# Attention steps of a graph network kernel: ScalarE makes the second half of the one-hots, VectorE the first, and the clamp of the logits goes

## The reference, cut to what matters

```python
e = leaky_relu(a_src[:, src] + a_dst[:, dst] + fc_b, 0.2)   # one row for each of 4 heads
seg_max = segment_max(e, src)
e = exp(e - seg_max[:, src])
seg_sum = segment_sum(e, src)
msg = (e / seg_sum[:, src])[:, :, None] * hp[:, dst, :]
agg = segment_sum(msg, src)                                  # mean over heads, + bias
```

## Time and profile before

| what | us |
| --- | --- |
| median of 3 runs | 20600.07 |
| lowest, highest | 20592.81, 20604.26 |
| the profiled execution | 20595.7 |
| its span in the trace | 20593.9 |
| of it the attention stage, first to last message (L2221) | 6272.9 to 8603.6 |
| VectorE busy in the whole span | 17281.9 (84%) |
| GpSimd busy | 13246.4 (64%) |
| TensorE busy | 9779.6 (47%) |
| ScalarE busy | 5966.3 (29%) |

### The profile page before, as it was taken

One profiled execution on the slowest core, in us unless ns is written; L12 is line 12 of the kernel. 1 busy time (PEld: TensorE's weight loads), 2 busy tenths in 40 slices (PEclk: granted clock), 3 DMA queues, 4 the chain that ended last, 5 costly groups with the idle time before them and its releaser, 6 DMA issues.

```text
span 20593.9 us, 293981 instructions
## 1 busy us (share of the span) xinstructions
PE 9779.6 (47%) x63545; PEld 7463.1 (36%) x63546; DVE 17281.9 (84%) x25284; ACT 5966.3 (29%) x13901; POOL 13246.4 (64%) x14067
## 2 busy tenths in 40 slices
PE   0114010110016777653348777777777765336432
PEld 0114010100015666643235555555555544225322
DVE  9989999999997888787659999999999986664666
ACT  0000333333322222230004444454545445004300
POOL 0058777777777777735757777777777731770376
PEclk9655555555558888755558888888888875555555
DMA  1033444444412112174331111111111147336534
GB/s 18 0 54 24 30 35 31 33 31 32 33 22 45 36 36 36 34 242 124 84 52 12 12 12 12 12 12 12 12 12 12 12 89 230 79 77 162 181 79 68
DMA packets 1751558, 1095.98 MB, mean 53 GB/s; under 512 B 1217323, under 2 KB 1658124, under 8 KB 1750028
## 3 DMA queue, kind: packets, MB, share of 16 engines
q0 software_dynamic: 454272, 412.11, 18.2%
q1 hardware_dynamic: 1089532, 417.46, 8.2%
q10 hardware_dynamic: 207632, 265.14, 4.1%
HBM read 700.94 MB, written 391.12 MB: 53 GB/s over the span
## 4 chain that ended last, share of the span: by engine, by line
DVE 43%; DVEq 20%; issue 12%; DMA 10%; PE 10%; POOL 3%; ACT 1%; ACTq 0%; POOLq 0%; SPq 0%
DVEq L2477 11%; DMA srcs<-spread,nbx 9%; DVE arena L1750 7%; DVE arena L1749 6%; DVE srcs L2472 6%; POOL srcs L801 3%; DVE red L2478 3%; PE banks L1264 2%; DVEq L2205 2%; PE banks L1347 2%; DVE arena L1722 2%; DVE arena L2173 2%; DVE arena L1567 2%; PE banks L1405 1%; PE banks L1193 1%
## 5 line engine op out<-in xcount | busy, mean ns | idle before, releaser
L779 POOL DMA_INDIRECT gat<-tab,nbr x3328 | 3509.4, 1054 | 2151.3 <-DMA nbr<-nbr_src 1137.2
L801 POOL DMA_INDIRECT srcs<-spread,nbx x2808 | 2654.9, 945 | 2713.5 <-DMA nbx<-from_src 1375.3
L779 POOL DMA_INDIRECT gat<-tab,pay x3328 | 3176.8, 955 | 1078.4 <-issue 854.3
L1405 PE MATMUL banks<-w2rows,dsts 128*128 128x384 f32 x6656 | 3177.9, 613 | 894.1 <-DVE srcs L2472 700.2
L745 POOL DMA_INDIRECT pay<-records,nbr x2560 | 2489.7, 973 | 797.7 <-issue 780.0
L2478 DVE TENSOR_REDUCE red<-srcs 128x80 f32<-128x1280 f32 x1664 | 2474.6, 1487 | 151.4
L2173 DVE TENSOR_TENSOR arena<-arena,banks 128x96 f32 (+2 forms) x4472 | 1210.4, 271 | 1474.0 <-PE banks L1264 890.6
L1193 PE MATMUL banks<-ident,arena 128*128 128x128 f32 x2240 | 426.3, 376 | 4231.5 <-DVE arena L1750 2810.2
L1264 PE MATMUL banks<-srcs,hot 128*128 128x96 bf16 (+1 forms) x11232 | 1148.5, 278 | 2482.7 <-DMA srcs<-spread,nbx 2364.0
L906 ACT COPY banks<-arena 128x1024 f32<-128x1024 f32 (+1 forms) x1508 | 1324.5, 879 | 3299.6 <-DVE arena L1750 1275.6
L1405 PEld LDWEIGHTS banks<-w2rows,dsts 128*128 128x128 f32 x6656 | 1359.9, 227 | 1735.0 <-DVE srcs L2472 849.2
(11 more groups left out here) (394 smaller groups left out, 20741.4 us busy)
## 6 DMA issues: line engine op xcount, KB each, us to landing
spread<-srcs SPq DMA_DIRECT2D x936, 192.0 KB
dsts<-key_rows SPq DMA_DIRECT2D x234, 512.0 KB, 4.1
spread<-srcs ACTq DMA_DIRECT2D x468, 204.0 KB
staged<-gat SPq DMA_DIRECT2D x416, 148.0 KB, 1.8
gat<-staged ACTq DMA_DIRECT2D x416, 148.0 KB
dsts<-key_rows ACTq DMA_DIRECT2D x117, 512.0 KB, 4.5
gat<-tab,nbr POOLq DMA_INDIRECT x3328
gat<-tab,pay POOLq DMA_INDIRECT x3328
```

The source lines that it names most:

```text
L779: pool.indirect_dma_start(out=gatv(s, GC[pas])[:, t, :], out_offset=None, in_=TAB[pas], in_offset=bass.IndirectOffsetOnAxis(ap=row, axis=0 ...
L801: pool.indirect_dma_start(out=chunk_rows(s, c)[:, q, :], out_offset=None, in_=rows, in_offset=bass.IndirectOffsetOnAxis(ap=nbx[:, r, s * X ...
L1405: last = t_.matmul(bank[1 + 2 * (p % 2) + h][:, 0:384], hid_rows[:, s % 2, 2 * p + h, :], w2rows[:, :], start=True, stop=True)
```

## The change

VectorE compares only tiles 0 to 3 of a step (512 elements) and still signals hot_ready. ScalarE makes tiles 4 to 7 in `second_hots`: it copies the four keys into an f32 tile `key_act`, waits for that (key_held), runs four `Abs` activations of 128 elements, waits for the last (hot_gap), and runs one `Relu` over 512 elements, which signals the new semaphore hot_second. TensorE's transposes wait for hot_ready and hot_second. `second_hots` for step n+2 stands at the end of ScalarE's step n, behind the two DMA issues, and its copy waits for the sums of step n-2, which read the same buffer. The first of ScalarE's 104 iterations is now written out. On VectorE the clamp is left out and the difference signals logit_ready itself.

```diff
+DVE_TILES = 4
@@ ScalarE
+            def second_hots(i, s, behind):
+
+                n = i * SLOTS + s
+                if behind:
+                    act.wait_ge(sums_ready, n - (SLOTS - 1))
+                s_.copy(key_act[:, :], key_att[:, bass.ds(i * (SLOTS * TPS) + (s * TPS + DVE_TILES), TPS - DVE_TILES)]).then_inc(key_held, 1)
+                act.wait_ge(key_held, n + 1)
+                for t in range(DVE_TILES, TPS):
+                    last = s_.activation(hot4[s][:, t, :], iota[:, :], ACT.Abs, bias=key_act[:, t - DVE_TILES:t - DVE_TILES + 1], scale=-1.0)
+                last.then_inc(hot_gap, 1)
+                act.wait_ge(hot_gap, n + 1)
+                second = hot4[s][:, DVE_TILES:TPS, :]
+                s_.activation(second, second, ACT.Relu, bias=ones[:, 0:1], scale=-1.0).then_inc(hot_second, 1)
+
@@ in attention_step(i, s, final, behind=True), at its end
                 if not (final and s >= 2):
                     attention_loads(i + (s + 2) // SLOTS, (s + 2) % SLOTS)
+                    second_hots(i + (s + 2) // SLOTS, (s + 2) % SLOTS, behind or s >= 2)
@@ TensorE
             def att_transposes(n, s):
                 pe.wait_ge(hot_ready, n + 1)
+                pe.wait_ge(hot_second, n + 1)
@@ VectorE
-                    one_hot(key_att, i + (s + 2) // SLOTS, s2, hot4[s2]).then_inc(hot_ready, 1)
+                    one_hot(key_att, i + (s + 2) // SLOTS, s2, hot4[s2][:, 0:DVE_TILES, :], DVE_TILES).then_inc(hot_ready, 1)
@@
-                v.tensor_tensor(logit[:, :, :], zz[:, 0, :, :], zz[:, 1, :, :], ALU.subtract)
-                dve.drain()
-                v.tensor_scalar(logit[:, :, :], logit[:, :, :], 0.0, None, ALU.min).then_inc(logit_ready, 1)
+                v.tensor_tensor(logit[:, :, :], zz[:, 0, :, :], zz[:, 1, :, :], ALU.subtract).then_inc(logit_ready, 1)
```

More of the change, by code:

```diff
@@ L274, in resnorm_gnn_kernel @@
         asrc = sb("asrc", [P, W, HEADS])
+        key_act = sb("key_act", [P, TPS - DVE_TILES])
         nodeam = sb("nodeam", [P, W, HEADS])
@@ L425, in resnorm_gnn_kernel @@
         hot_ready = sem("hot_ready")
+        hot_second = sem("hot_second")
+        key_held = sem("key_held")
+        hot_gap = sem("hot_gap")
         sums_ready = sem("sums_ready")
@@ L971, in attention_transposes, with attention_step @@
                 last.then_inc(hotT_ready, 1)
-            def attention_step(i, s, final):
+            def second_hots(i, s, behind):
[10 more added lines that the diff above has]
+                s_.activation(second, second, ACT.Relu, bias=ones[:, 0:1], scale=-1.0).then_inc(hot_second, 1)
+            def attention_step(i, s, final, behind=True):
                 n = i * SLOTS + s
@@ L982, in attention_step @@
                     attention_loads(i + (s + 2) // SLOTS, (s + 2) % SLOTS)
+                    second_hots(i + (s + 2) // SLOTS, (s + 2) % SLOTS, behind or s >= 2)
             attention_loads(0, 0)
             attention_loads(0, 1)
+            second_hots(0, 0, False)
+            second_hots(0, 1, False)
             attention_transposes(0, 0)
-            with act.Fori(0, ITERS - 1) as i:
+            for s in range(SLOTS):
+                attention_step(0, s, False, False)
+            with act.Fori(1, ITERS - 1) as i:
                 for s in range(SLOTS):
@@ L2158, in place_lanes, with one_hot @@
                 dve.drain()
[L2160 to L2163, removed]
+            def one_hot(key_tab, i, s, dst, tiles=TPS):
+                key = key_tab[:, bass.ds(i * (SLOTS * TPS) + s * TPS, tiles)]
+                return v.tensor_tensor(dst, lanes_p.rearrange("p (a n) -> p a n", a=1).to_broadcast([P, tiles, P]),
+                                       key.rearrange("p (t a) -> p t a", a=1).to_broadcast([P, tiles, P]),
                                        ALU.is_equal)
@@ L2227, in _ @@
             for s in range(2):
-                one_hot(key_att, 0, s, hot4[s]).then_inc(hot_ready, 1)
+                one_hot(key_att, 0, s, hot4[s][:, 0:DVE_TILES, :], DVE_TILES).then_inc(hot_ready, 1)
             for s in range(SLOTS):
```

## The result

The changed kernel took 21064.33 us (median of 4, 21058.29 to 21073.11) against 20599.65 us before (median of 4): 465 us more, a ratio of 1.0226 with a 95% interval of 1.0208 to 1.0244. The forecast was 21090. The profiled execution has a span of 21071.3 us, 477 us over that of before.

What follows compares the result with a forecast made beforehand. VectorE was taken to bound the kernel before, a two-step ring through TensorE after: 8.40 + 5.2 = 13.6 us, 6.80 a step, 1.19 more over 415 steps, 494 us, giving 21090. The 8-in-10 range was 20700 to 21170.

Steps and rivals of the forecast that it cites:

- VectorE bounds the kernel before: Attention stage: VectorE's own work of 5.616 us sets the step; ScalarE waits for its logits in all 416 steps.
- VectorE's savings: VectorE, each step: half a one-hot saves 0.53 us and the clamp 0.30, together 0.83.
- D: VectorE: from the start of one message to the end of the next step's last add, 4.86 us after the change.
- H: ScalarE: time from VectorE's last add to hot_second, summed to 3.45 us, with 3.1 and 3.8 as ends.
- T: TensorE's transposes of a step, said to wait for ScalarE's Relu in nearly all steps, about 3.4 us in longer ones.
- The ring: Two steps: last add, H, T and sums, next messages, VectorE's work to last add; 8.40 us plus the pair.
- At full clock no better than before: Attention stage: 8.40 + 2.95 = 11.35 us for two steps, 5.67 a step against 5.61.
- The clock: TensorE: its clock falls in the longer gap each time, slowing that pair to 5.2 us; stage clock about 0.75.
- pair: TensorE's T and sums together: 2.95 us at full clock, 4.57 with a fall within, 5.47 wholly slow.
- The rival of a clock that falls no more often: Attention stage: one pair in three at 4.57 us, as before; 5.94 us a step, 20733 us; chance 0.18.
- The rival that halves would be ready early: Attention stage: with H below 1.7 us only VectorE's 4.78 a step is left, 20252 us; faster side's chance 0.07.
- every pair would be wholly slow: TensorE, by the Trainium skill's rule alone: 8.40 + 5.47 = 13.87 us for two steps, 21144 us in all.

Runs made afterwards that it cites:

- no_clamp: Clamp left out of the kernel before, nothing else changed: 5.33 us a step, whole time 0.9944 of before.
- early: Changed kernel with ScalarE's one-hot half put ahead of its step's two DMA issues: 5.12 us a step, 0.9930 of before.
- swap: Changed kernel with TensorE doing the sums of step n-1 before the transposes of step n+1: 5.12 us a step, 0.9929 of before.
- fill16: Changed kernel plus 16 useless identity transposes on TensorE behind each step's node terms: 5.75 us a step, 1.0020 of before.
- after_again: The changed kernel, no edit, rerun on a chip of the experiments: 6.81 us a step, 1.0189 of before.
- split_clamp: Changed kernel with the clamp put back, so the split one-hots alone: 6.82 us a step, 1.0181 of before.
- late_tiles6: Changed kernel with ScalarE making 2 tiles instead of 4, still behind the DMA issues: 6.66 us a step, 1.0161 of before.
- early_fill16: Changed kernel with ScalarE's half ahead of the DMA issues and 16 useless transposes: 4.81 us a step, 0.9887 of before.

## Why the prediction was right, point by point

- **VectorE bounds the kernel before.** Right: no_clamp gave 0.28 us a step back for the 0.30 summed. The 0.03 for the clamp's slower run was no saving: without the clamp an idle 0.19 us stands before another instruction instead (19.1 us in all, 102 times).
- **VectorE's savings.** The half one-hot takes 0.68 us (0.69 in the row at 7401.16) instead of 1.22, 0.53 as summed. D from message to last add, 7399.99 to 7404.84, is 4.85 against 4.86.
- **H.** 3.45 in the sum, 3.51 as the median, 3.40 in the turn shown: copy 0.19 (0.21), four Abs 1.28 (1.27), Relu 0.72 (0.71, the value on the line through two lengths, not the 0.57 of halving). In the other half of the steps the Relu ends 4.1 to 4.4 us behind the last add, because ScalarE's copies wait for the slow T there. It costs little: that T stands behind the slow sums anyway, and at 7414.10 it had waited 0.33 us for the Relu. The handover from Relu to T is 0.14 us, not the 0.05 that the sum took from another pair of engines; D and H being a little short made up for it.
- **The ring.** Shown from both ends: with the place in ScalarE's order changed (early) or the order in TensorE's (swap), the step falls to 5.12.
- **At full clock no better than before.** Right: 5.67 summed, 5.75 in fill16, of which 0.04 is the longer handover (0.09 in two steps). VectorE's 0.83 went into a wait for TensorE, 373.1 us in that run.
- **The clock.** This step was argued from two rows and a neighbouring stage, and it held: a gap of 3.46 us, a pair of 5.21 (5.2 taken), the stage at 0.75, distances of 4.77 and 8.87 (4.8 and 8.8 said). fill16 makes it more than argued, since adding work removed 1.07 of the 1.20 us. The ring summed to 13.6 and measured 13.62 in the turn shown. That fit is partly luck: 5.2 was a choice between 4.57 and 5.47, and nothing in the rows of before fixed it. The same pair has a median of 5.21 us in the changed kernel, 5.01 in after_again, 4.87 in split_clamp and 5.48 in late_tiles6. In the first three it takes up what the rest of the ring leaves of about 13.65 us. With a mean clock of 0.75, TensorE spends half of that time at each of its two levels. Why two steps settle at this length no run here shows. What was predicted is that every second pair is slow and that a slow pair costs some 2 us on the ring.
- **The total.** 494 us were summed, 501 measured in the stage. The rest of the program gave back 24, the net of 6 us ahead of the stage and 30 behind it. Some of it can be named: of 2560 record gathers 274 lay behind the stage before the change and none after, and from the last message to the first chunk gather it is 797.8 instead of 804.7 us. The other 23 or so are spread over later stages by 2 to 7 us each, and I don't know their cause.
- **The rival of a clock that falls no more often** (5.94) was refuted on the chip: slow pairs are every second one, 0.50 of all instead of about a third. The rival that halves would be ready early is what early and early_fill16 built: early gave 5.12, since some pairs stay slow, and early_fill16 4.81, the 4.78 of that rival. That every pair would be wholly slow (13.87 us for two steps) did not happen: every second one ran at full clock, as that from 7414.10 to 7417.04, and in the slow pairs the clock came back before their end.

What was weak is the reason behind when and for how long the clock falls. It fitted the changed kernel, but the same reasoning missed late_tiles6 (6.1 for 6.66, a slow pair longer than taken), and it missed swap (6.0 for 5.12) and early (5.35 for 5.12) in the other direction: swap's clock was 0.95, and in early 91 of 414 pairs were slow, not every second or third.

## What to carry to other kernels

Work that is moved to an idle engine is judged by what releases it and who waits for it, not by the idle share: here the same activations at two places in ScalarE's order made the step 6.8 or 5.1 us. Where a new handover goes through TensorE, sum the ring of one and of several steps at both clock levels, since a ring that leaves TensorE idle can make its own matmuls slower (here 5.2 us instead of 2.9 for a pair behind a gap of 3.5 us). Before such an edit, look in TensorE's own order for what stands behind the instruction that will wait.

## What the hardware showed that I had not expected

- Useless matmuls made the kernel faster: 1.07 us a step for 16 of them (6.82 to 5.75), and only 0.23 for 8. In the kernel before they did nothing.
- Two steps add up to 13.65 us with the clamp and without it (8.58 + 5.07 and 8.90 + 4.75): once slow and fast pairs alternate, 0.3 us of VectorE's work more was made up for by a slow pair of 4.82 instead of 5.21 us.
- The kernel before took 20600 us in the first runs and 26275 to 26677 on the three chips of the experiments, while the changed kernel kept its step in the attention stage. The first message came at 6273 and 6279 us in the first runs and at 9799 to 9892 in the experiments, and the radial layer's one-hots spanned some 6030 us against 7440 to 7850. Its cause wasn't looked for.
